# Expert outputs added straight onto the result by accumulating indirect DMAs, pauses between GpSimd's late DMAs, and seven slot buffers laid in the key rows

## The chip, the cores and the metric

One core of one Trainium2 chip runs the kernel. The core has five engines that run their own programs and meet at semaphores: TensorE (PE) multiplies, VectorE (DVE) and ScalarE (ACT) work on rows, GpSimd (POOL) does simple operations and generates the descriptors of indirect DMAs, SyncE (SP) issues plain DMAs. The metric is the device time of one execution in microseconds (us), as the median of several runs.

## What is computed

A transformer block with 8 batches of 512 tokens of width 128: modulated layer norm, causal attention with 16 heads of 8, then a mixture of 8 experts with two choices per token and a capacity of 1024 tokens each.

```python
h = _layernorm(x) * (1 + ca) + sa
x = x + ga * attention(h)                       # per batch
h = _layernorm(x) * (1 + cb) + sb
logits = h @ Wr + br; topv, topi = top_k(logits, 2); gates = softmax(topv)
sel = one_hot(topi).sum(1); rank = cumsum(sel, axis=0) - sel; keep = (sel > 0) & (rank < cap)
# each expert e works on the (at most cap) tokens that it keeps:
out_e = gelu(xg_e @ W1[e] + b1[e]) @ W2[e] + b2[e]
final[token] += gate[token, e] * out_e          # two experts per token
x = x + gb * final
```

## The kernel before

**Attention.** The program of each engine is one list of steps n; a batch takes UB = 44 of them. Tables (`AT`, `SCATTER_AT`, `UP_AT` and so on) say at which step a piece of work is put into an engine's order. An engine runs its list strictly in order, waiting where a semaphore is not yet there. PE's order is made of scores (L613, L636), their product with the values (L663), and small pieces for the layer norms, the projection (L692) and routing (L701, L711, L722).

**Routing.** After attention of a batch, DVE works out each token's two experts, its rank in each, and the row of `slots_dram` (8 experts x 1024 rows of 258 floats: gb, h, gate, destination) that it goes to. GpSimd writes these rows with 8 indirect DMAs of 128 rows for a batch (`scatter`, L1583). The destination stored in a row is that token's row in `picks_dram`, which has two halves of 4096 rows: half 0 for the token's lower-numbered expert, half 1 for the other (`swap`, `tokid`). ACT fills `slots_dram` in advance with rows whose destination is out of bounds (32 DMAs) and `picks_dram` with zeros (8 DMAs of 512 KB).

**Experts.** 16 tiles of 512 slots: tiles 0 to 6 are the lower halves of experts 0 to 6, tiles 7 to 13 their upper halves, tiles 14 and 15 the two halves of expert 7. The last batch is ranked from the top end of the upper halves, so a lower half needs no row of batch 7. SP loads a tile's slots (`load_slots`, L452, 516 KB) into one of `SLOTS` = 5 buffers, which lie in `prob`, the buffer of attention's exponentials, and its expert's weights (`load_expert`, L461 and L462). PE transposes the rows (`slots_T`, L748), multiplies up (`up`, L738; 8 matmuls that leave 4 blocks), ACT applies gelu (L969), PE multiplies down (`down`, L758), DVE adds the bias (L1338) and multiplies by gate and gb (`gated`, L1353, 4 of them) into a ring of 4 output buffers `yout`, and GpSimd sends these with 4 indirect DMAs of 128 rows of 512 bytes to `picks_dram` (`send`, L1594). PE's order in the loop is up(t+1), transposes(t+2), down(t). Before the first transposes stand 22 idle matmuls (`WARM_AT`, L538).

**End.** When all sends have landed, SP loads both halves of `picks_dram` (16 loads, L524), DVE adds them to the attention's result `xall` (16 additions, L1377), and SP stores the output (8 stores, L527).

Of the kernel before, what the change touches and what calls it, by code (L numbers as in the profile page):

```python
# [17 lines left out]

# [3 lines left out]
F32 = mybir.dt.float32  # L22
BF16 = mybir.dt.bfloat16
U32 = mybir.dt.uint32
ALU = mybir.AluOpType
# [48 lines left out]
ZEROS = 8  # L74
SLOTS = 5
FILL_AT = [UB + 44 + 3 * i for i in range(FILLS)] + [UB + 154 + 13 * i for i in range(ZEROS)]

# [54 lines left out]
R_SEL, R_SWAP, R_IDS, R_DEN, R_ONE, R_TWO, R_RANK = 51, 50, 54, 53, 54, 63, 54  # L132
# [17 lines left out]
WARM_AT = [(15, 10), (15, 8), (23, 4)]  # L150
# [50 lines left out]
def adaln_moe_kernel(nc, x, wq, wk, wv, wo, wr, br, w1, b1, w2, b2, cT, wmod, out):  # L201
    ctx = ExitStack()
    with ctx:
# [3 lines left out]
        def sem(name):  # L207
# [7 lines left out]
        picks = nc.dram_tensor("picks_dram", [2 * N, C], F32).ap()  # L215
# [38 lines left out]
        tokid = sb("tokid", [P, 2, NT])  # L254
        vhalf = sb("vhalf", [P, NT])
        empty = sb("empty", [P, ROW])
        zeros = sb("zeros", [P, T])
# [34 lines left out]
        swap = sb("swap", [P, NT])  # L292
# [22 lines left out]
        two = kf.rearrange("p (b k j c) -> p b k j c", b=B, k=2, j=NT)  # L315
        slotin = prob[:, :, :].rearrange("p a t -> p (a t)")[:, 0:SLOTS * NT * ROW]\
            .rearrange("p (a j c) -> p a j c", a=SLOTS, j=NT)
# [7 lines left out]
        names = """maskrow_set x0_in x1_in x_in wqkv_in wo_in mod_w_in route_w_in b_in prefilled zeroed mod_stored modB_in  # L325
# [8 lines left out]
        r_log r_top1 r_eq1 r_pick1 r_best1 r_swap r_hot1 r_log2 r_top2 r_eq2 r_pick2 r_best2 r_hot2 r_sel  # L334
        g_gap g_exp g_den g_one g_two id_set rank_mm r_rank r_carry r_prod r_myrank r_myslot
        r_ahead r_over r_index scattered0 scattered1 id_next
        w_in0 w_in1 w_in2 w_in3 slot_in0 slot_in1 slot_in2 slot_in3 slot_in4 slot_tr slot_T hid_mm hid_done y_mm y_add y_done dest_done
        picked0 picked1 picked2 picked3 gb_in0 gb_in1 x2_low x2 out_done""".split()
        S = {n: sem(n) for n in names}
        two_in = [sem(f"two_in{b}") for b in range(0, B, 2)]  # L340
        low_in = [sem(f"low_in{b}") for b in range(0, B, 4)]
# [13 lines left out]
        def _(sp):  # L355
# [108 lines left out]
            def step(n):  # L464
# [21 lines left out]
                if b is not None:  # L486
                    copy_row(b)
                b = at(n, "load1")
# [25 lines left out]
            for t in range(4, 2 * E):  # L514
                if LOAD_OF[t] != LOAD_OF[t - 1]:
                    load_expert(LOAD_OF[t])
                if t >= SLOTS:
# [14 lines left out]
        def _(pe):  # L532
# [17 lines left out]
            pe.wait_ge(S["consts"], 7)  # L550
# [71 lines left out]
            def shifted(b, s):  # L622
# [16 lines left out]
                if b == B - 1:  # L639
                    if s == 0:  # L640
                        pe.wait_ge(S["consts"], 10)
# [214 lines left out]
        def _(act):  # L856
# [89 lines left out]
            def prefill(n):  # L946

                if n == 0:
                    act.wait_ge(S["consts"], 7)
                if n < FILLS:  # L950
# [733 lines left out]
```

## Time and profile before

| | |
|---|---|
| median of 3 runs | 561.09 us (558.45 to 562.75) |
| the profiled execution | 562.52 us, its span in the trace 560.8 us |
| busy share PE, DVE, ACT, POOL | 88%, 67%, 50%, 55% |
| mean granted TensorE clock | 0.942 of full speed |

Times in the trace count from the start of the span. "Idle before <- X" says what ended an engine's wait; "issue" or "remote" stand where the profile names no event that came just then. A matmul's end is modelled.

### The profile page before, as it was taken

How to read it: one execution, taken by the hardware profiler on the slowest of the kernel's cores; microseconds unless marked ns; L12 is line 12 of the kernel's file. 1: busy time of each engine (PE TensorE's matmuls, PEld its weight loads, DVE VectorE, ACT ScalarE, POOL GpSimd, SP SyncE). 2: the span in 40 equal slices, each digit the busy share in tenths (PEclk: the TensorE clock that was granted, in tenths of full speed). 3: DMA queues.
4: the chain of work that ended last, by engine and by line, in shares of the span. 5: the costliest groups of instructions: out<-in, count | busy, mean ns of one | idle time of the engine just before them, and what ended most of it. 6: DMA issues, size and time to landing. Idle time of an engine off the chain costs nothing.

```text
span 560.8 us, 11087 instructions
## 1 busy us (share of the span) xinstructions
PE 492.3 (88%) x3550; PEld 271.4 (48%) x3566; DVE 374.6 (67%) x1303; ACT 280.7 (50%) x527; POOL 308.5 (55%) x558
## 2 busy tenths in 40 slices
PE   8699898999999999999999998984995799999830
PEld 4233353455455445545545544432483477777630
DVE  3489887789999999999999996240352033333353
ACT  1400685676776776676776767572340243332200
POOL 4330454465487678688677776463217544545650
PEclk9979998999999999999999999986998799999965
DMA  3578877546644754753643504113615154643059
GB/s 87 169 217 215 286 221 210 164 165 190 163 164 125 221 163 153 202 181 85 165 134 79 138 11 117 52 45 117 206 57 160 60 171 141 190 139 108 7 182 298
DMA packets 70928, 83.48 MB, mean 149 GB/s; under 512 B 8330, under 2 KB 59303, under 8 KB 68438
## 3 DMA queue, kind: packets, MB, share of 16 engines
q1 hardware_dynamic: 54582, 61.69, 38.6%
q10 hardware_dynamic: 11168, 13.05, 7.1%
q0 software_dynamic: 5120, 8.04, 4.4%
q8 instruction: 28, 0.46, 0.4%
q14 instruction: 30, 0.25, 0.1%
HBM read 44.79 MB, written 35.80 MB: 144 GB/s over the span
## 4 chain that ended last, share of the span: by engine, by line
PE 50%; DVE 19%; issue 16%; DMA 5%; another core or an unknown queue 2%; POOL 2%; ACT 2%; SPq 1%; DVEq 1%; ACTq 0%; POOLq 0%
PE ps L613 9%; PE ps L663 8%; PE ps L758 8%; PE ps L738 8%; DVE ps L1125 7%; PE ps L636 7%; DMA qrows<-mT 2%; PE ps L538 2%; DVE negmax L1125 2%; PE ps L576 1%; DVE negmax L1129 1%; DMA krows<-k_dram 1%; PE ps L619 1%; PE ps L581 1%
## 5 line engine op out<-in xcount | busy, mean ns | idle before, releaser
L915 ACT ACTIVATE prob<-ps 128x512 f32<-128x512 f32 (+1 forms) x352 | 182.8, 559 | 88.7 <-PE ps L636 66.6
L1125 DVE CUSTOM_DVE_ANT_0 ps<-ps,maskrow 128x512 f32<-128x512 f32 (+1 forms) x256 | 155.9, 639 | 17.8 <-PE ps L613 16.5
L1546 POOL TENSOR_SCALAR_AFFINE_SELECT prob<-prob 128x128 f32<-128x128 f32 (+2 forms) x308 | 104.0, 348 | 75.1 <-ACT prob L915 69.9
L613 PE MATMUL ps<-krows,qrows 72*128 72x128 bf16 (+3 forms) x512 | 131.1, 307 | 11.0 <-DMA krows<-k_dram 3.9
L636 PE MATMUL ps<-qrows,krows 75*128 75x128 bf16 (+3 forms) x512 | 127.9, 303 | 4.5 <-DMA qrows<-mT 2.5
L1594 POOL DMA_INDIRECT picks_dram<-qrows,dest x64 | 62.7, 979 | 52.4 <-DVE qrows L1353 35.5
L663 PE MATMUL ps<-prob,vpad 128*32 128x128 f32 (+3 forms) x1024 | 88.9, 454 | 1.2 <-ACT oS L922 0.7
L613 PEld LDWEIGHTS ps<-krows,qrows 72*128 72x128 bf16 x512 | 45.5, 99 | 89.5 <-DVE negmax L1125 43.9
L969 ACT ACTIVATE qrows<-ps,b_sb 128x512 f32<-128x512 f32 x64 | 41.0, 688 | 91.4 <-PE ps L738 66.9
L1583 POOL DMA_INDIRECT slots_dram<-rows,index x64 | 64.9, 1013 | 26.5 <-issue 15.2
L738 PE MATMUL ps<-qrows,vpad 128*128 128x512 f32 x128 | 60.7, 616 | 9.1 <-ACT qrows L969 9.1
L1129 DVE TENSOR_REDUCE negmax<-ps 128x2 f32<-128x512 f32 (+1 forms) x96 | 61.4, 685 | 5.5 <-PE ps L619 5.1
L758 PE MATMUL ps<-vpad,qrows 128*128 128x128 f32 x512 | 61.8, 280 | 3.6 <-ACT qrows L969 3.0
L758 PEld LDWEIGHTS ps<-vpad,qrows 128*128 128x128 f32 x512 | 60.1, 196 | 5.2 <-issue 5.2
L636 PEld LDWEIGHTS ps<-qrows,krows 75*128 75x128 bf16 x512 | 46.8, 98 | 26.9 <-ACT prob L915 6.7
L1338 DVE TENSOR_TENSOR qrows<-ps,b_sb 128x512 f32<-128x512 f32 x15 | 10.4, 691 | 52.9 <-remote 30.2
L663 PEld LDWEIGHTS ps<-prob,vpad 128*32 128x32 f32 x1024 | 25.0, 110 | 41.2 <-issue 18.8
L738 PEld LDWEIGHTS ps<-qrows,vpad 128*128 128x128 f32 x128 | 23.6, 196 | 35.4 <-issue 28.8
L538 PE MATMUL ps<-onesb 128*128 128x512 bf16 x104 | 38.2, 458 | 2.3 <-POOL onesb L1462 2.2
L1125 DVE DVE_READ_ACCUMULATOR2_ANT negmax<- 128x1 f32 x256 | 36.6, 143 | 0.0
L1326 DVE COPY qrows<-ps 128x512 f32<-128x512 f32 x16 | 11.0, 689 | 33.7 <-remote 18.5
L1504 POOL TENSOR_SCALAR ln_var<-ln_mean 128x4 f32<-128x4 f32 x16 | 3.7, 230 | 50.8 <-DVE ln_mean L1095 50.6
(141 smaller groups left out, 542.8 us busy)
## 6 DMA issues: line engine op xcount, KB each, us to landing
qrows<-q_dram SPq DMA_DIRECT2D x48, 192.0 KB
krows<-k_dram SPq DMA_DIRECT2D x48, 192.0 KB
slots_dram<-empty ACTq DMA_DIRECT2D x32, 258.0 KB, 3.7
prob<-slots_dram SPq DMA_DIRECT2D x16, 516.0 KB
vpad<-in_w SPq DMA_DIRECT2D x30, 256.0 KB
k_dram<-kpart SPq DMA_DIRECT2D x40, 128.0 KB, 1.9
rows<-modB SPq DMA_DIRECT2D x8, 512.0 KB
picks_dram<-zeros ACTq DMA_DIRECT2D x8, 512.0 KB
```

The lines of the kernel that those rows point to most:

```text
L538: mm(ps[:, bank, :], onesb[:, :], onesb[:, None, :].to_broadcast([P, T // P, P]), start=True, stop=True)
L613: last = mm(bank[:, i * w:(i + 1) * w], qrows[0:SROWS, b % 2, h, qb * P:(qb + 1) * P], krows[0:SROWS, b % 2, h, 0:w], start=(i == 0), stop ...
L636: last = mm(bank[:, i * w:(i + 1) * w], krows[0:LROWS, b % 2, h, kind * P:(kind + 1) * P], qrows[0:LROWS, b % 2, h, kind * P:T], start=(i ...
L663: last = mm(ps[32 * grp:32 * grp + 32, OB, kind * P:T], vpad[:, b % 2, kind, head, :], prob[:, (half * UH + v) % PRING, i * w:(i + 1) * w] ...
L738: mm(ps[:, k, :], w1_sb[:, LOAD_OF[n] % 4, k * P:(k + 1) * P], slotT[:, n % 2, :], start=True, stop=True).then_inc(S["hid_mm"], 1)
L758: last = mm(ps[:, down_bank(n, j), j * P:(j + 1) * P], hid[:, n % 2, k, j * P:(j + 1) * P], w2_sb[:, LOAD_OF[n] % 4, k, :], start=(k == 0) ...
L915: fn(prob[:, s % PRING, 0:w], ps[:, TB + ring(s, TRING), 0:w], ACT.Exp, scale=SCALE)\
L1125: nc.vector.tensor_tensor_reduce(ps[:, SB_ + ring(s, SRING), 0:w], ps[:, SB_ + ring(s, SRING), 0:w], maskrow[:, T - w:T], -1.0, -NEG, ALU. ...
L1129: red(negmax[:, half, NT - 1 - kind, pos:pos + nh], ps[:, SB_ + ring(s, SRING), 0:nh * w].rearrange("p (n w) -> p n w", n=nh), AX.X, ALU.m ...
L1546: sel_(out=blk, in_=blk, compare_op=ALU.is_ge, fill=0.0, base=0, pattern=[[0, nh], [1, P]], channel_multiplier=-1).then_inc(S["masked"], 1)
L1583: pool.indirect_dma_start(slots, bass.IndirectOffsetOnAxis(index[:, u, k, j:j + 1], 0), rows[:, u, k, j, :], None, bounds_check=E * CAP - ...
L1594: pool.indirect_dma_start(picks, bass.IndirectOffsetOnAxis(dest[:, n % 8, j:j + 1], 0), yout[:, n % 4, j, :], None, bounds_check=2 * N - 1 ...
```

## The change

It has four parts.

1. `picks_dram` goes. After each batch's attention SP stores `xall` of that batch to the output (`store_x1`), and the sends add their rows onto the output in DRAM (`compute_op=ALU.add`). Two DMAs that add onto the same row must not overlap: a token has two experts, so a send waits until the sends of the last two tiles, where they are of another expert, have landed. The first one waits for all 8 stores. The loads, additions and stores at the end go, and with them the zero fill (8 DMAs of ACT), the `swap` operation and one of two operations on the ids.
2. `pause`: a memset of 128x384 floats on GpSimd, which waits for the memset of the pause before. One stands behind every scatter DMA from batch 5 on and one in the middle of each send. GpSimd's sequencer so cannot run further ahead than one pause.
3. The slot buffers become seven and lie in `krows`, the key rows of attention. Tiles 0 to 2 are loaded when the keys of batch 6 have been read and batch 6's scatters have landed; they no longer wait for the last copy of attention's sums (`o_copied`). Tiles 3 to 5 are loaded behind the copy of batch 7's rows.
4. The 22 idle matmuls (`WARM_AT`) go.

```diff
-SLOTS = 5
+SLOTS = 7
+PAUSE_FROM = 5
-WARM_AT = [(15, 10), (15, 8), (23, 4)]
+WARM_AT = []
-        slotin = prob[:, :, :].rearrange("p a t -> p (a t)")[:, 0:SLOTS * NT * ROW]\
-            .rearrange("p (a j c) -> p a j c", a=SLOTS, j=NT)
+        slotin = kf[:, 0:SLOTS * NT * ROW].rearrange("p (a j c) -> p a j c", a=SLOTS, j=NT)
...
+            def store_x1(b):
+
+                sp.wait_ge(S["x1_done"], b + 1)
+                sp.dma_start(out[b].rearrange("(j p) c -> p j c", p=P), xall[:, b]).then_inc(S["x1_out"], 16)
...
+                else:
+                    sp.wait_ge(S["maxed"], UB * (B if t >= 3 else B - 1))
+                    sp.wait_ge(S["shifted"], UB * (B if t >= 3 else B - 1))
...
                 if n == SHIFT + UB * B + SLOT_IN_AT:
+                    for t in range(3):
+                        load_slots(t)
                     sp.wait_ge(S["o_copied"], 2 * B)
-                    for t in range(SLOTS):
+                    load_expert(2)
+                if n == place("row_b", B - 1) + 1:
+                    load_slots(3)
+                    load_expert(3)
+                    for t in range(4, FIRST_TILES):
                         load_slots(t)
-                        if 2 <= t < 4:
-                            load_expert(t)
...
-            pv = picks.rearrange("(k b p j) c -> b k p j c", k=2, b=B, p=P)
-            for k, tiles in ((0, 2 * E - 2), (1, 2 * E)):
-                for z in range(4):
-                    sp.wait_ge(S[f"picked{z}"], 16 * NT * ((tiles + 3 - z) // 4))
-                for b in range(B):
-                    sp.dma_start(two[:, b, k], pv[b, k]).then_inc(two_in[b // 2] if k else low_in[b // 4], 16)
-            for b in range(B):
-                sp.wait_ge(S["x2"], b + 1)
-                sp.dma_start(out[b].rearrange("(j p) c -> p j c", p=P), xall[:, b]).then_inc(S["out_done"], 16)
-            sp.wait_ge(S["out_done"], 16 * B)
+            sp.wait_ge(S["x1_out"], 16 * B)
+            for z in range(4):
+                sp.wait_ge(S[f"picked{z}"], 16 * NT * ((2 * E + 3 - z) // 4))
...
+            def pause():
+
+                z = next(pauses)
+                if z > 1:
+                    pool.wait_ge(S["paused"], z - 1)
+                ms(spare[:, :], 0.0).then_inc(S["paused"], 1)
...
                                         oob_is_err=False).then_inc(S[f"scattered{b % 2}"], 16)
+                if b >= PAUSE_FROM:
+                    pause()
...
                 if not earlier(n):
-                    pool.wait_ge(S["zeroed"], 16 * ZEROS)
+                    pool.wait_ge(S["x1_out"], 16 * B)
                 pool.wait_ge(S["dest_done"], n + 1)
+                for back in (1, 2):
+                    if earlier(n, back) and TILES[n - back][0] != TILES[n][0]:
+                        pool.wait_ge(S[f"picked{(n - back) % 4}"], 16 * NT * ((n - back) // 4 + 1))
                 for j in range(NT):
                     pool.wait_ge(S["y_done"], NT * n + j + 1)
-                    pool.indirect_dma_start(picks, bass.IndirectOffsetOnAxis(dest[:, n % 8, j:j + 1], 0),
-                                            yout[:, n % 4, j, :], None, bounds_check=2 * N - 1,
-                                            oob_is_err=False).then_inc(S[f"picked{n % 4}"], 16)
+                    pool.indirect_dma_start(result, bass.IndirectOffsetOnAxis(dest[:, n % 8, j:j + 1], 0),
+                                            yout[:, n % 4, j, :], None, bounds_check=N - 1, oob_is_err=False,
+                                            compute_op=ALU.add).then_inc(S[f"picked{n % 4}"], 16)
+                    if j == 1:
+                        pause()
```

**GpSimd, from batch 7's last scatters into the sends, after the change.** `slots_dram<-rows,index` is a scatter, `out<-qrows,dest` a send (the `yout` ring lies in `qrows`), `spare` the memset of a pause.

```order
302 L1565 DMA slots_dram<-rows,index 8192x258
303 L1551 MEMSET spare 128x384 [waits paused]
306 L1581 DMA out<-qrows,dest 4096x128 [waits y_done,dest_done,x1_out]
307 L1581 DMA out<-qrows,dest 4096x128 [waits y_done]
308 L1551 MEMSET spare 128x384 [waits paused]
309 L1581 DMA out<-qrows,dest 4096x128 [waits y_done] x2
310 L1565 DMA slots_dram<-rows,index 8192x258
311 L1551 MEMSET spare 128x384 [waits paused]
312 L1581 DMA out<-qrows,dest 4096x128 [waits y_done,picked0,dest_done]
316 L1581 DMA out<-qrows,dest 4096x128 [waits picked0,y_done,picked1,dest_done]
```

Before, the same stretch has the same DMAs without the memsets, and a send waits for `y_done` and `dest_done` alone. Now send 1 waits for send 0 (`picked0`), send 2 for sends 0 and 1, and so on to send 14.

**SP, where the first slots are loaded, before the change.** `prob<-slots_dram` is a load of a tile's slots, `vpad<-in_w` one of an expert's weights, `rows<-rows` the copy of batch 7's rows.

```order
194 L452 DMA prob<-slots_dram 128x4x258 [waits scattered1,scattered0,o_copied]
195 L452 DMA prob<-slots_dram 128x4x258 [waits scattered1,scattered0] x2
196 L461 DMA vpad<-in_w 128x512
198 L452 DMA prob<-slots_dram 128x4x258 [waits scattered1,scattered0]
199 L461 DMA vpad<-in_w 128x512
201 L452 DMA prob<-slots_dram 128x4x258 [waits scattered1,scattered0]
203 L442 DMA rows<-rows 128x4x128 [waits scattered1,h2_b]
```

**The same place after the change**, where `krows<-slots_dram` is the load of slots and `out<-xall` the store of a batch's attention result.

```order
201 L456 DMA krows<-slots_dram 128x4x258 [waits scattered0,scattered1,shifted,maxed] x3
202 L465 DMA vpad<-in_w 128x512 [waits o_copied]
205 L438 DMA rows<-rows 128x4x128 [waits scattered1,h2_b]
206 L443 DMA out<-xall 128x4x128 [waits x1_done]
207 L456 DMA krows<-slots_dram 128x4x258 [waits scattered0,scattered1,shifted,maxed]
208 L465 DMA vpad<-in_w 128x512
210 L456 DMA krows<-slots_dram 128x4x258 [waits scattered0,scattered1,shifted,maxed] x2
```

The first three loads no longer wait for `o_copied`; the next three moved behind the copy of batch 7's rows and the store of its result.

## Rows read from the trace of the kernel before

**Rows 1.** The page, part 1: busy time, share of the span, instructions.

```profile
PE 492.3 (88%) x3550; PEld 271.4 (48%) x3566; DVE 374.6 (67%) x1303; ACT 280.7 (50%) x527; POOL 308.5 (55%) x558
```

**Rows 2.** Chain that ended last, in order of time: start us, us, what. Its end.

```profile
542.86 2.54 DMA picks_dram<-qrows,dest
...
547.73 5.27 DMA krows<-picks_dram
...
554.79 0.80 DVEq L203
```

**Rows 3.** The same chain in the loop over tiles.

```profile
456.15 3.44 PE ps L738 x8
...
463.60 3.44 PE ps L738 x8
...
519.59 3.59 PE ps L758 x32
```

**Rows 4.** Timeline 376 to 398: start us, us, engine, line, operation [idle before].

```profile
380.57 0.27 PE L663 MATMUL ps<-prob,vpad 128*32 128x128 f32 x1 [0.50 <-issue]
...
383.89 0.98 POOL L1583 DMA_INDIRECT slots_dram<-rows,index  x1 [0.30 <-issue]
386.45 0.60 ACT L922 ACTIVATE oS<-ps 128x512 f32<-128x512 f32 x1 [7.66 <-remote]
387.07 1.48 SPq L452 DMA_DIRECT2D prob<-slots_dram  x3
...
390.16 6.71 PE L538 MATMUL ps<-onesb 128*128 128x512 bf16 x22
...
397.60 0.60 PE L748 MATMUL ps<-ident,prob 128*128 128x128 f32 x4
```

**Rows 5.** Stretches: us, busy of PE, PEld, DVE, ACT, POOL, PEclk, DMA share, GB/s.

```profile
392.00:394.00 2.00, 2.00 (x7) 0.72 (x6) 0.00 (x0) 0.51 (x2) 0.00 (x0) 0.55 1.08 361
```

**Rows 6.** Timeline 415 to 446: batch 7's scatters and the first sends.

```profile
418.97 1.12 POOL L1583 DMA_INDIRECT slots_dram<-rows,index  x1 [3.98 <-DVE rows L1266]
...
424.24 3.60 PE L738 MATMUL ps<-qrows,vpad 128*128 128x512 f32 x8
...
428.04 0.97 POOL L1594 DMA_INDIRECT picks_dram<-qrows,dest  x1 [0.30 <-issue]
...
433.24 0.97 POOL L1583 DMA_INDIRECT slots_dram<-rows,index  x1 [0.30 <-issue]
434.07 0.69 ACT L969 ACTIVATE qrows<-ps,b_sb 128x512 f32<-128x512 f32 x1 [16.46 <-issue]
...
443.51 0.60 PE L748 MATMUL ps<-ident,prob 128*128 128x128 f32 x4
```

**Rows 7.** Timeline 455 to 480: one tile of the loop.

```profile
458.26 1.14 DVE L1353 SCALAR_TENSOR_TENSOR qrows<-qrows,prob 128x128 f32<-128x128 f32 x4
...
459.44 0.97 POOL L1594 DMA_INDIRECT picks_dram<-qrows,dest  x1 [2.88 <-DVE qrows L1353]
...
463.28 0.97 POOL L1594 DMA_INDIRECT picks_dram<-qrows,dest  x1 [0.30 <-issue]
...
465.20 0.69 DVE L1338 TENSOR_TENSOR qrows<-ps,b_sb 128x512 f32<-128x512 f32 x1 [4.37 <-remote]
```

**Rows 8.** Timeline 354 to 366: an ordinary GpSimd operation between scatters of batch 5.

```profile
362.95 0.47 POOL L1524 TENSOR_TENSOR wo_ga<-wo_sb,modB 128x128 f32<-128x128 f32 x1
...
364.56 1.27 ACT L915 ACTIVATE prob<-ps 128x512 f32<-128x512 f32 x2 [2.89 <-PE ps L643]
```

**Rows 9.** Timeline 0 to 30, GpSimd: the longest plain memset near the pause's size.

```profile
2.13 0.53 POOL L1464 MEMSET zeros<- 128x512 f32 x1
```

**Rows 10.** DMA issues over the span: names, queue, count, KB each, us to landing.

```profile
k_dram<-kpart SPq DMA_DIRECT2D x40, 128.0 KB, 1.9
...
krows<-picks_dram SPq DMA_DIRECT2D x16, 256.0 KB, 4.3
...
cT_sb<-in_cT ACTq DMA_DIRECT2D x1, 4.0 KB, 2.5
```

More of the change, by code:

```diff
@@ L17 @@
 from contextlib import ExitStack
+from itertools import count
 import concourse.bass as bass
@@ L73 @@
 FILLS = 32
-ZEROS = 8
-SLOTS = 5
-FILL_AT = [UB + 44 + 3 * i for i in range(FILLS)] + [UB + 154 + 13 * i for i in range(ZEROS)]
+SLOTS = 7
+PAUSE_FROM = 5
+FILL_AT = [UB + 44 + 3 * i for i in range(FILLS)]
 def width(kind):
@@ L214, in adaln_moe_kernel @@
         slots = nc.dram_tensor("slots_dram", [E * CAP, ROW], F32).ap()
-        picks = nc.dram_tensor("picks_dram", [2 * N, C], F32).ap()
+        result = out.rearrange("b t c -> (b t) c")
         xall = sb("xall", [P, B, NT, C])
@@ L333, in adaln_moe_kernel @@
         s2_bn s2_var s2_v s2_rstd s2_norm h2_a h2_b rows_b0 rows_b1 h2T_tr h2T_copied logit_mm
[L334 removed]
+        r_log r_top1 r_eq1 r_pick1 r_best1 r_hot1 r_log2 r_top2 r_eq2 r_pick2 r_best2 r_hot2 r_sel
         g_gap g_exp g_den g_one g_two id_set rank_mm r_rank r_carry r_prod r_myrank r_myslot
         r_ahead r_over r_index scattered0 scattered1 id_next
[L337 to L338 removed]
+        w_in0 w_in1 w_in2 w_in3 slot_in0 slot_in1 slot_in2 slot_in3 slot_in4 slot_in5 slot_in6 slot_tr slot_T hid_mm hid_done y_mm y_add y_done dest_done
+        picked0 picked1 picked2 picked3 gb_in0 gb_in1 paused x1_out""".split()
         S = {n: sem(n) for n in names}
[L340 to L341 removed]
         block = ctx.enter_context(nc.Block())
@@ L487, in step @@
                     copy_row(b)
+                    store_x1(b)
                 b = at(n, "load1")
@@ L948, in prefill @@
                 if n == 0:
-                    act.wait_ge(S["consts"], 7)
-                if n < FILLS:
-                    z = slice(n * (E * CAP // P // FILLS), (n + 1) * (E * CAP // P // FILLS))
-                    act.dma_start(slots.rearrange("(p n) c -> p n c", p=P)[:, z, :],
-                                  empty[:, None, :].to_broadcast([P, E * CAP // P // FILLS, ROW]))\
-                        .then_inc(S["prefilled"], 16)
-                else:
-                    z = slice((n - FILLS) * (2 * N // P // 4 // ZEROS), (n - FILLS + 1) * (2 * N // P // 4 // ZEROS))
-                    act.dma_start(picks.rearrange("(p n m) c -> p n (m c)", p=P, m=T // C)[:, z, :],
-                                  zeros[:, None, :].to_broadcast([P, 2 * N // P // 4 // ZEROS, T]))\
-                        .then_inc(S["zeroed"], 16)
+                    act.wait_ge(S["consts"], 6)
+                z = slice(n * (E * CAP // P // FILLS), (n + 1) * (E * CAP // P // FILLS))
+                act.dma_start(slots.rearrange("(p n) c -> p n c", p=P)[:, z, :],
+                              empty[:, None, :].to_broadcast([P, E * CAP // P // FILLS, ROW]))\
+                    .then_inc(S["prefilled"], 16)
             def gelu(n):
@@ L1251, in route @@
                         dve.wait_ge(S[f"scattered{b % 2}"], 16 * 2 * NT * (b // 2))
-                    for k in range(2):
-                        stt(rows[:, u, k, :, DEST], swap[:, :], float(N - 2 * N * k), tokid[:, k, :],
-                            ALU.mult, ALU.add).then_inc(S["id_set"], 1)
+                    cp(rows[:, u, :, :, DEST], tokid[:, None, :].to_broadcast([P, 2, NT])).then_inc(S["id_set"], 1)
                 if s == R_DEN:
@@ L1368, in finish @@
                     gated(n, j)
-            def add(b, k):
-                if k:
-                    dve.wait_ge(two_in[b // 2], 32)
-                    dve.wait_ge(S["x2_low"], b + 1)
-                elif b % 4 == 0:
-                    dve.wait_ge(low_in[b // 4], 16 * 4)
-                tt(xall[:, b], xall[:, b], two[:, b, k], ALU.add).then_inc(S["x2" if k else "x2_low"], 1)
             def step(n):
@@ L1447, in _ @@
                 finish(t)
-            for k in range(2):
-                for b in range(B):
-                    add(b, k)
         @block.gpsimd
@@ L1566, in next_ids @@
             def next_ids(b):
-                pool.wait_ge(S["id_set"], 2 * (b + 1))
-                ts(tokid[:, :, :], tokid[:, :, :], float(T), None, ALU.add).then_inc(S["id_next"], 1)
+                pool.wait_ge(S["id_set"], b + 1)
+                ts(tokid[:, :], tokid[:, :], float(T), None, ALU.add).then_inc(S["id_next"], 1)
+            pauses = count(1)
+            def pause():
[3 more added lines that the diff above has]
+                ms(spare[:, :], 0.0).then_inc(S["paused"], 1)
             def scatter(b, n):
```

32 lines of the change are left out of this document (11 added, 21 removed).

## Prediction

> **What bounds the kernel now.** I read the page's busy times first. PE is busy 88% of the span [rows 1], but that is an average over stages. So I went through the chain of work that ended last, and then through timelines of the places where it leaves PE. There are four stages to see.
>
> (a) In the loop over tiles PE runs without a break: up(6) starts at 456.15, the next up at 463.60, so a tile takes 7.45 us, and down(13) ends at 523.18 [rows 3]. GpSimd has slack there: a tile's first send starts at 459.44 and its last at 463.28 [rows 7], and the next tile's comes a period after the first.
>
> (b) At the end the last send starts at 542.86 and has landed 2.54 us later. The loads of the second half, the additions and the stores follow, until 560.8 [rows 2]. That is 15.4 us after the landing.
>
> (c) In two places every engine but GpSimd stands still while GpSimd issues DMAs back to back. PE's last product of attention ends at 380.84, but ACT, which needs it, starts at 386.45, just after the last of 8 scatters (383.89 + 0.98 = 384.87) [rows 4]. And up(3) has run on PE by 427.84, but ACT's gelu of it starts at 434.07 after 16.46 us of waiting. PE is back in order only at 443.51, when the transposes that follow up(4) start, though up(4) is 3.6 us of work [rows 6]. That hole is 443.5 - 427.8 - 3.6 = 12.1 us. I read it like this: what PE signals reaches the others late while GpSimd has a run of four or more DMAs going. Even in the loop DVE takes up a finished down only at 465.20, 0.95 us after the last send's end [rows 7].
>
> (d) Between attention and experts SP issues the first slot loads at 387.07. PE fills the time with 22 idle matmuls from 390.16 to 396.87 and starts the first transposes at 397.60 [rows 4].
>
> **The change, part by part.**
>
> *The end.* The loads, additions and stores go: 15.4 us, less about 1 us in which SP sees the last landing and the program closes (the closing row is 0.80 us [rows 2]).
>
> *Slots and warm-up.* In the kernel before, the slot loads waited for ACT's copy, which ended at 387.05, as well as for the scatters. Now the scatters alone count. They get 7 pauses. A memset of 512 floats is 0.53 us [rows 9], so one of 384 is about 0.40. It starts where 0.30 us of gap stood [rows 4], and some 0.16 us stays behind it, so I take +0.27 us a pause (from 0.1 to 0.45), 1.9 us in all. Less ACT's stall in batch 5's scatters (2.89 us [rows 8]), that leaves the loads at about 387, as before. A 256 KB load from DRAM lands in 4.3 us [rows 10]; at that the first transposes can start near 391.4, 6.2 us before 397.60. The cover that the idle matmuls gave is gone: the granted clock was 0.55, the lower level of 1.2 GHz for most of it, up to 394 [rows 5], so PE begins the first up at half speed. If it takes as long from its start as from 390.16 to 394, it loses about 1.2 us. Gain: 5 us for PE, from here to 424. DVE's chain to batch 7's scatters moves with it, as its copy of the first transposed slots stands ahead of batch 7's residual addition: they start at 414 instead of 418.97.
>
> *Pauses at the first sends.* 7 scatters at 1.28 + 0.27 = 1.55 us take until 424.8, send 0 (4 x 1.28 + 0.27 = 5.4 us) until 430.2, the eighth scatter until 431.8. Send 1 starts near 432. If the pauses let PE's signals through, the 12.1 us hole closes, and up(6) starts at 456.15 - 5 - 12.1 = 439. PE would then finish down(13) at 506, and the gated rows of tile 14 would be there by 515.
>
> *The chain of landings.* This is the wait that the change adds, and it sets the end. Behind the waiting send stand all later sends, and for them wait DVE (the ring of 4) and SP's last wait. A send starts when the one before has landed. From gated row to first DMA takes 459.44 - 458.55 = 0.85 us (458.26 and the first of four in 1.14 us) [rows 7]; the last DMA starts 3 x 1.28 + 0.27 = 4.1 us later; then comes the landing, L. So the period is P = 4.95 + L. Sends 1 to 14 make 13 periods; 15 waits for 13 only and follows 14 directly. The end is
>
> 432 + 13 x (4.95 + L) + 5.4 + 4.1 + L + 1 = 506.9 + 14 L.
>
> L of a plain send is 2.54 with a DMA_INDIRECT of 1.28 us, so about 2.2 with the usual 0.97 [rows 2, 7]. An adding DMA must also read its destination from DRAM; no row shows one. From below: nothing added, 2.2. From above: a whole small read (4 KB in 2.5 us [rows 10]) ahead of the write, 4.7. The nearest pair is a store from SBUF, 1.9 us, and a small load from DRAM, 2.5 us [rows 10]: 0.6 us for the source being in DRAM. I take 2.2 + 0.6 = 2.8, with some load traffic 2.9. With that P is 7.85 us, above PE's 7.45: GpSimd's chain becomes the bound, and part of the gain of PE is not seen. The end is 506.9 + 40.6 = 547.5 us. The profiled span before is 560.8 and the median 561.09, so I say 548.
>
> The Trainium skill ("DMA: Bandwidth & Descriptors", Anatomy of one DMA) gives a GpSimd DMA 2.0 us fixed plus bytes over 436 GB/s, an estimate of 2.15 us for 64 KB whatever the operation; the sum would then be 537. The last send's row, 2.54, is somewhat above that. The skill's "Collectives: The Full Stack" (Part 3) speaks against the change: an add in the DMA's path needs two source reads and two read descriptors for each piece. No trace of before shows whether that costs here.
>
> *The rest.* The 8 stores of `xall` (256 KB each) move into attention's time; the zero fill and final stores, 6.3 MB, go. ACT's 8 issues, the `swap` and one id operation go too. I cost them at nothing: the work beside them is PE's; if that cover were gone, SP's extra issue is about 0.5 us a batch (1.48 us for three [rows 4]), 4 us in all.
>
> **Rivals.**
>
> 1. *The landing is short.* With L of 2.2 to 2.5, the period is at or under PE's 7.45: 537 to 542. For it: a send moves 512-byte rows only. Against: the read.
> 2. *The pauses don't do what they are for.* Rows 8 speak for it: a 0.47 us operation at 362.95 between scatters let ACT go only at 364.56, 1.1 us after it ended. Then the 12.1 us hole stays and the gated rows of tile 4 come at 454, where send 4 by the chain starts at 432 + 3 x 7.85 = 455.5. The chain hides it; it costs the stall at 381 and stretches in the loop, 2 to 8 us: 550 to 556.
> 3. *The chain just eats the gain.* L of 3.5 to 4.2: 556 to 566.
> 4. *Slower.* Above L = 4.3 the end is over 567. The two-read rule would do the same in another way: if issuing takes GpSimd longer for two read descriptors, each 0.1 us on a DMA counts about 50 times on the chain, 5 us. With 0.5 us more (half of 0.97 again) and L = 2.9 the end is 573, with L = 3.5, 581. It decides from 0.4 us a DMA. For it: 13 landings in series, none overlapped; against: plain DMAs of 1032-byte and 512-byte rows both take about 0.97 us, so the time is in the 128 descriptors' making, and only the reading half of it would grow.
>
> **How the numbers follow.** The forecast (L 2.5 to 3.5) has 0.40 and a range of its own from 542 to 555; rival 1 0.14; rival 2 0.12; rival 3 0.14; rival 4 0.20. About 1% is what a measurement of this kernel can tell from no change, so faster means under 555.5 and slower over 566.7: faster 0.40 + 0.14 + 0.12 = 0.66, same 0.14, slower 0.20. The range from 536 to 573 leaves out about half of rival 4 and the corner below rival 1.
>
> **What the profile after would show.** Step by step: the end falls within 2 us of the last send's landing. The first transposes stand near 391. No hole of over 3 us on PE between 420 and 440. The wait before a tile's first send is ended by the landing of the send before, not by DVE, and first sends are 7.85 us apart; where they are 7.45 apart, PE is still the bound and rival 1 holds. A DMA_INDIRECT of a send is 0.97 us long, else rival 4. The forecast is wrong if the landing takes under 2.5 or over 3.5 us, since each 0.1 us there is 1.4 us at the end.

## The result and the profile after

The changed kernel takes 588.35 us (median, 587.66 to 594.32) where the kernel before, timed beside it, takes 559.77 (558.21 to 562.75). The ratio is 1.0527 with a 95% interval from 1.0442 to 1.0613: slower by 5%. The forecast was 548 us, and even its range ended at 573. In what follows a ratio leaves out the executions that came over 1.5% above the fastest of their kernel, while a median and the range behind it keep them.

The page of the changed kernel, parts 1, 3 and 5 (busy us, share, instructions; packets, MB, share; busy us, mean ns, idle before and its releaser):

```profile
PE 488.2 (83%) x3544; PEld 269.7 (46%) x3544; DVE 364.0 (62%) x1271; ACT 282.5 (48%) x527; POOL 361.4 (62%) x597
...
q0 software_dynamic: 12288, 8.05, 7.9%
...
L1581 POOL DMA_INDIRECT out<-qrows,dest x64 | 99.9, 1560 | 49.2 <-DVE qrows L1339 28.4
...
L1339 DVE SCALAR_TENSOR_TENSOR qrows<-qrows,krows 128x128 f32<-128x128 f32 x64 | 18.6, 347 | 62.6 <-DMA out<-qrows,dest 62.2
```

PE's share falls from 88% [rows 1] to 83%, GpSimd's busy time rises from 308.5 to 361.4 us. The third row tells most of it: a send's DMA is 1560 ns long, where one before took 970 ns [rows 6, 7], and 64 of them make some 37 of the 53 us; most of the rest are the memsets of the pauses. DVE waits 62 us in all for landings, since the ring of four `yout` buffers is emptied late.

Timeline of GpSimd in the loop, two tiles (start us, us, what, idle before):

```profile
443.09 1.55 POOL L1581 DMA_INDIRECT out<-qrows,dest  x1 [2.68 <-issue]
444.94 1.55 POOL L1581 DMA_INDIRECT out<-qrows,dest  x1 [0.30 <-DVE qrows L1339]
445.91 1.01 POOL L1551 MEMSET spare<- 128x384 f32 x1
447.09 1.56 POOL L1581 DMA_INDIRECT out<-qrows,dest  x1 [0.17 <-issue]
448.95 1.55 POOL L1581 DMA_INDIRECT out<-qrows,dest  x1 [0.30 <-issue]
454.06 1.57 POOL L1581 DMA_INDIRECT out<-qrows,dest  x1 [3.55 <-DVE qrows L1339]
```

From a tile's first DMA to its last are 448.95 - 443.09 = 5.86 us, and from there to the next tile's first 5.11, in which the last one lands. The same place in [rows 7] held four DMAs in 4.8 us and no wait for a landing. The profile puts the last wait down to DVE, but that isn't what the send waited for. DVE itself had just been released by the same landing, to fill the buffer that became free:

```profile
453.33 1.14 DVE L1339 SCALAR_TENSOR_TENSOR qrows<-qrows,krows 128x128 f32<-128x128 f32 x4 [2.49 <-DMA out<-qrows,dest]
```

These rows are for tile 6; the rows of the waiting send 3 had been ready for long. In the semaphore updates that the trace holds, the landing of send 2 is complete at 453.23, that is 4.28 us after its last DMA's start, and GpSimd starts the next send 0.82 us later. This last step, from a landing to the next DMA, is called dispatch below. And the end:

```profile
561.24 1.55 POOL L1581 DMA_INDIRECT out<-qrows,dest  x1 [0.30 <-issue]
565.08 1.55 POOL L1581 DMA_INDIRECT out<-qrows,dest  x1 [2.30 <-issue]
...
572.81 1.55 POOL L1581 DMA_INDIRECT out<-qrows,dest  x1 [0.30 <-issue]
...
578.67 1.55 POOL L1581 DMA_INDIRECT out<-qrows,dest  x1 [0.30 <-issue]
```

565.08 is send 14. Send 1 started at 432.86, so 13 periods (a period runs from one send's first DMA to the next one's) took 132.2 us, 10.17 each. The one shown above is among the longest, 10.97 us. The span ends at 585.9, 7.2 us after the last DMA's start. Nothing of [rows 2] behind the landing is left.

What stood in the way before is gone. Stretches of the changed kernel, then of the kernel before, over the hole of [rows 6] (us; busy of PE, PEld, DVE, ACT, POOL; PEclk, DMA share, GB/s):

```profile
427.00:444.00 17.00, 17.00 (x99) 12.39 (x99) 6.36 (x18) 5.87 (x9) 11.93 (x10) 1.00 0.61 152
```

```profile
427.00:444.00 17.00, 7.93 (x15) 2.56 (x15) 1.83 (x5) 2.75 (x4) 13.04 (x14) 0.70 0.33 107
```

How late PE's signals were can be read from the trace. In the kernel before, down(2) ends on PE at 424.40, but the update of the semaphore that it signals is recorded at 430.47, and DVE, which waits for it, starts at 430.49:

```profile
430.49 0.69 DVE L1338 TENSOR_TENSOR qrows<-ps,b_sb 128x512 f32<-128x512 f32 x1 [7.51 <-remote]
```

From the end of a block of an up product on PE to the start of ACT's gelu of it are up to 14.0 us there (up(3)). In the changed kernel none of the 64 takes over 1.4 us. This delay is the measure by which the experiments below are compared; the ends of products in it are modelled by the profile.

And the answers to [rows 4] in the changed kernel: ACT's wait, the slot loads and the first transposes.

```profile
376.25 0.60 ACT L924 ACTIVATE oS<-ps 128x512 f32<-128x512 f32 x1 [1.66 <-PE ps L665]
...
383.44 1.47 SPq L456 DMA_DIRECT2D krows<-slots_dram  x3
...
387.30 1.12 PE L750 MATMUL ps<-ident,krows 128*128 128x128 f32 x4 [6.15 <-DMA krows<-slots_dram]
```

So PE got its early gain and more. It was lost again behind GpSimd.

### The profile page after: what moved, and what is told of

The parts are those of the page before. It is cut to its first block and busy times, and to the rows that moved or that the text cites. A ratio compares the mean times of both kernels' runs of the same rounds, so it can differ in the third digit from the quotient of the medians.

```text
span 585.9 us, 11041 instructions
## 1 busy us (share of the span) xinstructions
PE 488.2 (83%) x3544; PEld 269.7 (46%) x3544; DVE 364.0 (62%) x1271; ACT 282.5 (48%) x527; POOL 361.4 (62%) x597
## 3 DMA queue, kind: packets, MB, share of 16 engines
q0 software_dynamic: 12288, 8.05, 7.9%
## 5 line engine op out<-in xcount | busy, mean ns | idle before, releaser
L1121 DVE CUSTOM_DVE_ANT_0 ps<-ps,maskrow 128x512 f32<-128x512 f32 (+1 forms) x256 | 155.6, 636 | 19.9 <-PE ps L615 18.4
L1581 POOL DMA_INDIRECT out<-qrows,dest x64 | 99.9, 1560 | 49.2 <-DVE qrows L1339 28.4
L965 ACT ACTIVATE qrows<-ps,b_sb 128x512 f32<-128x512 f32 x64 | 43.6, 687 | 89.3 <-PE ps L740 87.9
L1565 POOL DMA_INDIRECT slots_dram<-rows,index x64 | 64.9, 1014 | 22.9 <-issue 13.4
L740 PE MATMUL ps<-qrows,vpad 128*128 128x512 f32 x128 | 63.7, 646 | 7.2 <-issue 7.2
L1339 DVE SCALAR_TENSOR_TENSOR qrows<-qrows,krows 128x128 f32<-128x128 f32 x64 | 18.6, 347 | 62.6 <-DMA out<-qrows,dest 62.2
L740 PEld LDWEIGHTS ps<-qrows,vpad 128*128 128x128 f32 x128 | 25.3, 207 | 35.2 <-issue 35.2
L540 PE MATMUL ps<-onesb 128*128 128x512 bf16 x82 | 29.8, 429 | 2.2 <-POOL onesb L1436 2.2
L621 PE MATMUL ps<-mask,identb 128*128 128x256 bf16 (+1 forms) x96 | 29.7, 309 | 0.0
```

The costliest lines, as they stand in the source:

```text
L740: mm(ps[:, k, :], w1_sb[:, LOAD_OF[n] % 4, k * P:(k + 1) * P], slotT[:, n % 2, :], start=True, stop=True).then_inc(S["hid_mm"], 1)
L965: fn(hid[:, n % 2, k, :], ps[:, k, :], ACT.Gelu, bias=b1_sb[:, NF * TILES[n][0] + k:NF * TILES[n][0] + k + 1]).then_inc(S["hid_done"], 1)
L1121: nc.vector.tensor_tensor_reduce(ps[:, SB_ + ring(s, SRING), 0:w], ps[:, SB_ + ring(s, SRING), 0:w], maskrow[:, T - w:T], -1.0, -NEG, ALU. ...
L1565: pool.indirect_dma_start(slots, bass.IndirectOffsetOnAxis(index[:, u, k, j:j + 1], 0), rows[:, u, k, j, :], None, bounds_check=E * CAP - ...
L1581: pool.indirect_dma_start(result, bass.IndirectOffsetOnAxis(dest[:, n % 8, j:j + 1], 0), yout[:, n % 4, j, :], None, bounds_check=N - 1, o ...
```

## The experiments

Kernels that were timed together form a series, always with the kernel before beside them, which stood at 557 to 568 us from series to series. Ratios are to the kernel before in the same series. In one series (e2_add_free, h_wait, a_no_pause, h_every) the kernel before spread from 553.31 to 567.88 us around its median of 561.93, too widely for a ratio, so only its times are given; a difference of 1% from it says nothing there. h_every lies below its lowest, a_no_pause above its highest. The experiments are in four groups: what an add costs, what each part does alone, what in the pauses works, and what is left then.

### What an add costs

**e1_plain_out**: the changed kernel with plain writes, so the sum x1 + y is left out; order, waits and pauses stay.

```diff
-                                            yout[:, n % 4, j, :], None, bounds_check=N - 1, oob_is_err=False,
-                                            compute_op=ALU.add).then_inc(S[f"picked{n % 4}"], 16)
+                                            yout[:, n % 4, j, :], None, bounds_check=N - 1, oob_is_err=False).then_inc(S[f"picked{n % 4}"], 16)
```

> The changed kernel with its sends as plain indirect writes onto the output (no add, so of two experts' rows the later one stays and attention's result is overwritten); waits, pauses, slots as in the change. Theory A (the add itself is dear: it makes a send's DMA_INDIRECT 1.56 us instead of 0.97, and its landing longer): DMA_INDIRECT goes back to 0.97 us, first sends of tiles come at PE's pace of about 7.45 us, the span is 538 to 548. Theory B (the DMAs are long because of where they write, or because of the waits in front of them, and the chain of waits alone makes the period of 10.2 us): DMA_INDIRECT stays near 1.56 us, or the period stays over 9 us, and the span stays over 575.

Measured: 545.33 us (544.16 to 546.22), ratio 0.975 [0.969, 0.981]. Its timeline:

```profile
458.80 0.97 POOL L1581 DMA_INDIRECT out<-qrows,dest  x1 [2.09 <-issue]
460.07 0.97 POOL L1581 DMA_INDIRECT out<-qrows,dest  x1 [0.30 <-DVE qrows L1339]
461.03 0.44 POOL L1551 MEMSET spare<- 128x384 f32 x1
461.64 0.97 POOL L1581 DMA_INDIRECT out<-qrows,dest  x1 [0.17 <-issue]
462.92 0.97 POOL L1581 DMA_INDIRECT out<-qrows,dest  x1 [0.30 <-issue]
465.86 0.97 POOL L1581 DMA_INDIRECT out<-qrows,dest  x1 [1.97 <-issue]
...
535.26 0.97 POOL L1581 DMA_INDIRECT out<-qrows,dest  x1 [0.30 <-issue]
```

The period shown is 465.86 - 458.80 = 7.06 us. Over the same 13 periods the mean is 7.36 us, 2.8 less than with the add. 1.7 of them are the issue (4.2 instead of 5.9 us from a send's first DMA to its last, on average), 1.1 the landing: by the semaphore updates it takes 2.3 us on average, 2.1 to 3.3, where the adding one takes 3.45, 2.7 to 4.4. Dispatch is 0.83 us, the same. The span is 542.4. By the ratios, 0.975 against 1.053 in another series, this one word of the change, `compute_op`, costs some 43 us. Theory B, that the waits or the place written to make the DMAs long, is out.

**e2_add_free**: the add without its waits. The kernel before with pauses and slots, whose sends add into `picks_dram` (its rows are zero) and wait for no landing.

```diff
-                                            oob_is_err=False).then_inc(S[f"picked{n % 4}"], 16)
+                                            oob_is_err=False, compute_op=ALU.add).then_inc(S[f"picked{n % 4}"], 16)
```

> The kernel before with the pauses and the slots, and with its sends adding onto picks_dram, whose rows are zero, instead of writing them; it has no waits on landings, so it holds the adding instruction without the chain. Theory A (GpSimd's issuing of an add is dear by itself): each of the 64 sends shows about 1.56 us instead of 0.97 us, a tile of four costs GpSimd 4 x 1.86 + 0.27 = 7.7 us, so sixteen tiles from 432 end near 555, and with the final loads, adds and stores of some 15 us the span is 568 to 576. Theory B (an add is dear only where GpSimd waits for landings between tiles): the sends show about 1.0 us and the span is 548 to 560, as with the pauses and slots alone.

Measured: 568.48 us (567.84 to 571.98) beside 561.93, profiled span 566.6.

```profile
L1615 POOL DMA_INDIRECT picks_dram<-qrows,dest x64 | 99.9, 1561 | 17.0 <-issue 15.6
```

Theory A holds to the number: 1561 ns, with no landing waited for; what idle time there is, is the 0.17 to 0.30 us between two instructions. PE is busy 20.00 us in each stretch of 20 from 400 to 500, so only GpSimd is behind: its 64 sends start from 422.8 to 546.8, 7.9 us a tile. So even with no chain the add alone makes GpSimd slower than PE's 7.45 us a tile [rows 3]; the chain of landings adds 2.3 us a tile to that.

### Each part alone

**b_slots** and **b_pauses** put one part each on the kernel before, **h_both** puts both, all with plain sends and the old end.

```diff
-SLOTS = 5
+SLOTS = 7
-WARM_AT = [(15, 10), (15, 8), (23, 4)]
+WARM_AT = []
```

```diff
+                if b >= PAUSE_FROM:
+                    pause()
...
+                    if j == 1:
+                        pause()
```

> The kernel before with the seven slot buffers in the key rows, the three early loads and no idle matmuls; no pauses, no adds (the low half of the sums at the end is loaded into the exponentials' buffer). PE starts the first transposes some 3 to 6 us earlier, but the hole near 430 stays: 553 to 558. If the missing idle matmuls cost more than the earlier loads bring: 560 to 565.

> The kernel before with the pauses alone (behind each scatter from batch 5 on, and in the middle of each send); sends write to the two halves and are added at the end, as before. If back-to-back DMAs on GpSimd hold back what PE signals, and pauses let it through: the hole of 12.1 us on PE near 430 goes, ACT's wait of 7.7 us near 386 shrinks to under 3, and the span is 538 to 548. If the pauses only lengthen GpSimd's work and the hole closed in the changed kernel for another reason (the slots that came earlier): 558 to 566, hole still there.

> The kernel before with pauses and slots, that is, the change without its adding sends. Theory A: both gains add up, 532 to 541, so the adding sends cost the changed kernel about 45 to 50 us. Theory B as for the plain writes would still let this one be fast; a span over 555 would say that pauses and slots bring nothing here and the loss of the change is not the adds' alone.

Measured: b_slots 560.92 us, 1.000 [0.995, 1.005]; b_pauses 554.51, 0.991 [0.986, 0.995]; h_both 555.32, 0.989 [0.981, 0.998]. The slots bring nothing, although PE starts its first transposes at 388.54: the hole stays, PE works only 11.94 us of the stretch from 420 to 440. The pauses gain, but at most half of what was expected (6.8 us against 13 and more), and pauses and slots together gain no more than the pauses alone, where 20 us and more had been expected. In b_pauses ACT's wait ahead of oS is gone (1.67 us before the start at 382.64), yet a slow stretch follows later, at a granted clock of 0.83, where ACT takes up PE's products 9.5 to 10.0 us late:

```profile
440.00:460.00 20.00, 16.82 (x76) 11.69 (x75) 5.11 (x14) 5.28 (x8) 14.43 (x18) 0.83 0.48 146
```

**h_wait** is h_both with the changed kernel's waits for landings, plain sends and the old end.

```diff
+                for back in (1, 2):
+                    if earlier(n, back) and TILES[n - back][0] != TILES[n][0]:
+                        pool.wait_ge(S[f"picked{(n - back) % 4}"], 16 * NT * ((n - back) // 4 + 1))
```

> The kernel before with the pauses, the slots and the waits for the landings of the last two tiles, with plain writes into picks_dram and the final additions kept. Theory A (what makes TensorE slow near 450 to 462 with pauses and slots alone is that GpSimd issues without a gap, and a wait of GpSimd opens one): TensorE runs its tiles without the stretch of single matmuls, the sends go 7.2 us apart as with plain writes onto the output, the last starts near 535, and with some 13 us behind it the span is 546 to 552. Theory B (waits for landings only cost time): the last send starts later than before, at 545 or more, and the span is 557 to 565.

Measured: 559.51 us (557.16 to 560.95) beside 561.93. The mechanism of theory A is there: PE is busy 20.00 of 20 in each stretch from 400 to 500, with nothing of the slow stretch and no delay of ACT over 1.8 us, while GpSimd stands idle some 2 us a tile. The time isn't, and its profiled span of 556.7 us is close to theory B's range: the last send starts at 538.3, not 535, and the old end behind it takes 18.4 us, not the 13 that were reckoned.

**a_no_pause** is the changed kernel without pauses.

```diff
-PAUSE_FROM = 5
+PAUSE_FROM = 8
...
-                    if j == 1:
-                        pause()
```

> The changed kernel without any of its pauses. Theory A (in the loop the waits for landings already give gaps, so pauses there only cost; before the loop the scatters' pauses matter): the period of a tile falls from 10.17 us by one pause's 0.27 us to 9.9 us, four us less over the loop, but the scatters of batches 5 to 7 hold TensorE and ScalarE back again near 380 to 390, by some 6 us; GpSimd's chain begins at most 2 us later, and the time is 0.990 to 1.005 of the changed kernel's, 582 to 591. Theory B (the pauses carry the changed kernel as a whole): holes of 10 us return on TensorE and the time is 595 or more.

Measured: 583.71 us (579.18 to 590.20) beside 561.93. That is theory A's range; the changed kernel had 588.35 in another series, so whether its pauses cost anything there isn't told by these two. ACT's wait ahead of oS is back, and during batch 7's scatters ACT takes up PE's products 5 us late; in the loop, without any pause, no delay is over 1 us:

```profile
379.51 0.60 ACT L924 ACTIVATE oS<-ps 128x512 f32<-128x512 f32 x1 [7.69 <-remote]
```

### What in a pause works

**h_every** has a pause after each DMA of a send, **h_two** after the second and the fourth, **h_tiny** after each, but every pause (of the scatters too) is of one column instead of 384. All else is h_both. The edits, in this order (h_tiny has that of h_every as well):

```diff
-                    if j == 1:
-                        pause()
+                    pause()
```

```diff
-                    if j == 1:
+                    if j % 2:
                         pause()
```

```diff
-                ms(spare[:, :], 0.0).then_inc(S["paused"], 1)
+                ms(spare[:, 0:1], 0.0).then_inc(S["paused"], 1)
```

> As the kernel with pauses and slots, but with a pause after each of a send's four DMAs instead of after the second. Theory A (a pause lets through the signals that TensorE's work waits for or that wait for it): every stretch with TensorE at single matmuls between 440 and 462 goes, a tile of sends costs GpSimd 4 x 1.57 = 6.3 us, below TensorE's 7 us, and the span is 543 to 549. Theory B (a pause of 0.44 us is no gap; only an idle GpSimd lets them through): the slow stretch stays or grows, and the span is 553 to 562.

> Pauses after the second and the fourth DMA of every send, so no more than two DMAs stand together: a tile costs GpSimd 5.7 us. Theory A (two DMAs together are short enough): no slow stretch on TensorE, the last send near 519.5 and the span 536 to 541. Theory B (every DMA needs its pause): a slow stretch near 445 to 462 and the span 548 to 556.

> As the kernel with a pause after every scatter from batch 5 on and after every DMA of a send (544.8 us), but each pause sets one column instead of 384. Theory A (the pause works by its length, some 0.4 us in which GpSimd writes no descriptors): the shorter pause lets less through, TensorE shows the slow stretches or holes again near 430 to 460, and the time is 552 to 562 us. Theory B (any instruction with a wait between two indirect DMAs is enough): GpSimd issues faster and the time is 541 to 546 us.

Measured: h_every 544.84 us (542.83 to 545.64) beside 561.93, and once more in another series (h_again, below) 0.974 [0.964, 0.983]; h_two 553.63, 0.981 [0.971, 0.990]; h_tiny 555.80, 0.994 [0.990, 0.999]. So h_every and h_tiny came out as their theories A said, h_two as its theory B. h_two stood in one series with h_again, and all its executions (553.06 to 555.40) are above all of h_again (546.78 to 551.35). Two stretches of h_every, then the worst one of h_two and of h_tiny:

```profile
420.00:440.00 20.00, 20.00 (x102) 13.22 (x101) 5.39 (x15) 9.50 (x14) 17.86 (x27) 1.00 0.52 163
440.00:460.00 20.00, 20.00 (x127) 15.38 (x126) 7.40 (x19) 6.33 (x10) 17.89 (x26) 1.00 0.54 169
```

```profile
440.00:460.00 20.00, 16.08 (x69) 10.50 (x69) 3.13 (x8) 3.07 (x5) 15.63 (x20) 0.83 0.36 109
```

```profile
420.00:440.00 20.00, 12.74 (x47) 7.49 (x48) 2.60 (x7) 5.39 (x8) 13.71 (x26) 0.74 0.29 90
```

GpSimd is busier in h_every than in the others, and PE never stops; ACT takes up no product over 1.4 us late. In h_two it is up to 6.9 us, in h_tiny up to 10.3. h_tiny has as many instructions, in the same order with the same waits, but the old spacing, as the short memset fits in the gap that stood there anyway:

```profile
429.81 0.97 POOL L1615 DMA_INDIRECT picks_dram<-qrows,dest  x1 [0.19 <-issue]
430.77 0.13 POOL L1588 MEMSET spare<- 128x1 f32 x1
431.08 0.97 POOL L1615 DMA_INDIRECT picks_dram<-qrows,dest  x1 [0.19 <-issue]
```

```profile
438.08 0.97 POOL L1615 DMA_INDIRECT picks_dram<-qrows,dest  x1 [0.17 <-DVE qrows L1363]
439.04 0.44 POOL L1588 MEMSET spare<- 128x384 f32 x1
439.65 0.97 POOL L1615 DMA_INDIRECT picks_dram<-qrows,dest  x1 [0.17 <-issue]
```

The first is h_tiny, 1.27 us from DMA to DMA, with the hole; the second is h_every, 1.57, without it. So an instruction with a wait between two DMAs isn't enough to let PE's signals through; the DMAs must come further apart, or the memset must run for some time. e2_add_free speaks for the distance: its DMAs follow each other with the same gap of 0.30 us as those of the kernel before, but being longer they start 1.86 us apart, with one pause in four, and no delay of ACT is over 1.4 us. At two DMAs together (h_two) some of the gain is already lost.

### What is left then

**b_every** and **b_front** have the five slot buffers and the idle products of before, **h_front** and **h_again** the seven. b_every and h_again pause after every DMA; in the two "front" kernels only sends 0 to 5 do, the later ones pause after their second DMA.

```diff
-                    if j == 1:
+                    if j == 1 or n < 6:
                         pause()
```

> The kernel before with a pause after every scatter from batch 5 on and after every DMA of a send, with its own five slot buffers and idle products. Theory A (with the hole gone, the earlier slots are worth what they save at the loop's start): the first transposes come 7 to 10 us later than with the slots, and the time is 549 to 555 us, some 6 to 9 us above the kernel with both. Theory B (the slots are worth nothing, as they were alone): 543 to 547 us.

> Pauses and slots as in the kernel with a pause after every DMA (544.8 us), but from send 6 on only the pause after the second DMA. In that kernel GpSimd issues without a wait from 424 to 527, 64 sends 1.57 us apart, and its last send starts at 525.9 where TensorE's last products end at 514. Theory A (the early sends need the pauses, later ones only make GpSimd late): six tiles cost 6.28 us and ten 5.4 us, the last send starts near 519.5 behind TensorE, and the span is 536 to 540. Theory B (four DMAs with one pause between them hold TensorE's signals back whenever GpSimd is behind): a slow stretch on TensorE appears after 463 and the span is 545 to 555.

> The same pauses as in the kernel with pauses to send 5, on the five slot buffers and the idle products of before. Theory A (the slots are worth what they save at the loop's start, 4.8 us at the first transposes, as the batch-7 scatters start 4.4 us earlier with them): this kernel is 3 to 5 us above h_front. Theory B (the slots are worth nothing): within 1.5 us of it.

> The kernel with slots and a pause after every DMA once more, beside the three others on one chip: 541 to 547 us, and the last send near 526. If it stands within 1 us of h_front, GpSimd's late sends weren't what ended it.

Measured: b_every 542.43 us, 0.970 [0.959, 0.982], in one series with h_tiny; and in another series h_front 547.22, 0.970 [0.959, 0.981], b_front 548.29, 0.971 [0.959, 0.983], h_again 549.36, 0.974 [0.964, 0.983]. None of these four is told apart from another. The last sends, of h_front, h_again and b_front:

```profile
524.99 0.97 POOL L1615 DMA_INDIRECT picks_dram<-qrows,dest  x1 [0.30 <-issue]
```

```profile
527.37 1.20 POOL L1615 DMA_INDIRECT picks_dram<-qrows,dest  x1 [0.17 <-issue]
```

```profile
528.43 1.27 POOL L1608 DMA_INDIRECT picks_dram<-qrows,dest  x1 [0.51 <-issue]
```

h_front was expected to send last at 519.5 and h_again to take 541 to 547 us; neither did, though the kernel before was at its slowest in this series (568.01). b_front came out as its theory B said, and b_every 0.6 us under the range of its own. With the fewer pauses in h_front PE loses a little in each later stretch (19.15, 19.05 and 17.46 us busy of 20 from 460 on) and its last products end at 518.4. At 475 ACT takes up products 6.2 us late there. Fewer pauses make GpSimd faster and PE slower by about the same. The slots shift all of it by 3.4 us in the profiled executions (528.43 against 524.99), but only by 1.1 us in the medians, less than their spread.

So the version that beats both kernels is the kernel before with pauses of 0.44 us after every late DMA of GpSimd, plain sends and the old end (b_every): 3% faster than before and, 0.970 against 1.053, some 8% faster than the changed one. The interval of the 3% is from 2 to 4; with the slots the same pauses stand at 0.974 (h_again). It needs neither the adds nor, as far as these runs can tell, the slots.

## Why the prediction was wrong, step by step

**What bounds the kernel: right.** The reading of [rows 4] and [rows 6], that PE's signals come late while GpSimd issues without a break, is borne out by the semaphore update at 430.47, 6.1 us after its product's end, and by h_tiny and h_every, which differ in nothing but the memset's width. Why an indirect DMA holds them back stays open.

**The issue of an adding send: the step that failed.** The prediction took a send's DMA at 0.97 us, as a plain one, with 1.28 from start to start, and so put what the add costs GpSimd at nothing. It is 1.56, and 1.86 from start to start. That turns "the last DMA starts 4.1 us later" into 5.86: +1.76 us in each of 13 periods, 22.9 us, +2.3 in send 14 (7.73 for 5.4), +1.8 in the last tile. 27 of the 38 us between 547.5 and 585.9 are this term. No other would have made the kernel slower: with the landing and the close as they were measured (below) the prediction's sum gives 506.9 + 14 x 3.45 + 2.9 = 558 us. e2_add_free shows it without any chain, e1_plain_out shows it gone. Rival 4 had named the mechanism and its price rightly (0.6 us on a DMA by its 5 us for each 0.1 is 30); the error was to hold it unlikely. "Only the reading half of it would grow" was the argument against it. But if half of 0.97 us doubles, that is 0.49 us more, above the 0.4 from which this rival decides: the argument spoke for it.

The Trainium skill, "Collectives: The Full Stack" (Part 3), says of the reduce of a collective that it emits two read descriptors for each chunk. No run here shows how many reads a send's add makes. What the trace shows is that more pieces go through GpSimd's queue: 5120 packets before and 12288 after, 112 more for each of the 64 sends, while the bytes stay at 8.05 MB. The packets of 4096 bytes that carried eight rows each are gone, and 512-byte packets of one row stand in their place. With that the issue of a DMA grew by 0.59 us.

**The landing.** The term L = 2.9 was too small, but inside the 2.5 to 3.5 that the forecast allowed: 3.45 us on average over the 13 periods, with 0.82 of dispatch where 0.85 was taken. Over 13 periods the excess is 10.17 - 7.85 - 1.76 = 0.56 us each, 7.3 us. Little of it is the traffic beside it. Sends 8 to 13 start after 505, where the loads are over (15 GB/s from 500 to 540), and still land in 3.0 to 3.4 us, 3.3 on average; sends 1 to 7 take 3.6 on average, and only two of them over 4. The plain landing was read rightly: "about 2.2" came out as 2.24 us for e1_plain_out's last send. So what was sized too small is what the add does to a landing: 0.6 us was taken from the pair of a store and a load, and it is 1.1.

**The close.** "L + 1" after the last DMA's start, 3.9 us, was 7.2. By the semaphore updates the last landing came at 581.97, so L was 3.3, and 3.9 us followed until the program ended. It isn't the add's: e1_plain_out needs 542.4 - 535.3 = 7.1 us from there as well, though its last landing took 2.24 us only. So these 7 us don't follow the landing, and what sets them stays open. Before, the last indirect DMA was 18 us from the end, and its row gave no hint of this. +0.4 and +2.9, 3.3 us in all.

**The removed end: right.** Loads, additions and stores, 15.4 us, are gone, and x1's stores cost nothing: PE is busy 20.00 of 20 in e1_plain_out from 400 to 500.

**The slots: right on the trace, wrong on the time.** The transposes came at 387.30, earlier than 391.4, as SP issued at 383.44 and not 387: batch 6's scatters start at 369.96, where they started at 374.83 before, and end earlier than forecast. The removed idle products cost more than the 1.2 us taken: the first up ran 6.11 us instead of 3.60, at a granted clock of 0.50 up to 394. Batch 7's scatters started at 411.46 (forecast 414). But b_slots is at 1.000 [0.995, 1.005] and b_front within 1.1 us of h_front. What PE gained there should have passed on to the end; with the slots alone it ran into the hole.

**The pauses: right in size, half right in effect.** 1.57 us from scatter to scatter (forecast 1.55), and no hole: up(6) started at 435.06 (forecast 439). But part of that was the chain's doing. With the same pauses and plain sends (b_pauses) the hole came back as a slow stretch, and h_wait shows the landing waits taking it away. Rival 2, that pauses don't do it, was thus right for plain sends without waits and pauses as sparse as these; with one after every DMA (h_every) they do it.

**The chain: right in form.** Send 1 started at 432.86 (forecast 432), and each period is issue, landing, dispatch, though the profile names DVE at most of these waits. With plain sends it is 7.36 us, under PE's 7.45 [rows 3]; the add moves it to 10.17.

## What to carry to other kernels

An indirect DMA that adds costs GpSimd 1.6 times a plain one here: multiply that by all sends before counting what a removed final pass saves, and if sends must follow one another's landings, count the landing beside the traffic of that stage. When a rival mechanism has a price by which it decides the sign, and the argument against it ("only half would grow") leaves more than that price, give it the larger chance. Where other engines stop while GpSimd issues DMAs in a row, see that every two of them really move apart, here by a memset of 0.44 us after each DMA. One after every second or fourth DMA gave only part of it.

## What the runs showed of the hardware that was not expected

- A 128-row indirect DMA of 512-byte rows with an add takes GpSimd 1.55 to 1.56 us, against 0.97 plain, whether it waits for anything or not (e2_add_free). It makes 112 more packets, as its rows travel one by one in 512-byte packets and no longer eight in one of 4096.
- It lands 3.0 to 3.4 us after its start where nothing else loads, and up to 4.4 beside loads; a plain one 2.1 to 2.3, and up to 3.3 beside loads (e1_plain_out). GpSimd starts the send that waits for it 0.82 us later.
- DMAs of GpSimd 1.27 us from start to start hold PE's signals back (PE busy 12.74 of 20 us), at 1.57 us they don't (20.00 of 20), with the same instructions. Whether the memset's own run or only the time matters wasn't tried by itself; e2_add_free, 1.86 us apart with one memset in four, has no such delay.
- A program whose last work is an indirect DMA of GpSimd ends 7.1 to 7.2 us after that DMA's start, adding or plain.
